# Slot steps and LoRA splits on GpSimd, and a new order at the start of z, in a quantized-weight and expert kernel

## What is computed

```python
lora_delta = lora_B @ lora_A * (LORA_ALPHA / LORA_RANK)
scale = jnp.exp(scale_log)
normalized = (weight + lora_delta).reshape(O, I // GROUP, GROUP) / scale
idx = jnp.searchsorted(thresholds, normalized, side='left')
quantized = cb[idx]
w_q = (quantized * scale).reshape(O, I)
x = x + x @ (w_q + lora_delta).T              # L0
W = weights[itok_B_0_15]
x = x + jnp.einsum('bct,bcd->bdt', x, W)      # L1
```

## Time and profile before

| | |
|---|---|
| median of 3 runs | 78.94 us (78.63 to 78.97) |
| the profiled execution | 78.95 us |
| its span | 77.1 us |
| granted TensorE clock | 1.0 in all slices |
| TensorE, VectorE, ScalarE, GpSimd busy | 71.6, 55.6, 47.3, 4.6 us |
| HBM read, written | 5.89 MB, 4.19 MB |

### The profile page before, as it was taken

The page is one execution under the profiler, slowest core; times in us unless marked ns, Lnnn a source line. Parts: engine busy times, 40 slices in busy tenths (PEclk is TensorE's granted clock), DMA queues, the critical chain, the costliest instruction groups (busy, mean ns, idle before and its releaser), DMA issues.

```text
span 77.1 us, 1130 instructions
## 1 busy us (share of the span) xinstructions
PE 71.6 (93%) x382; PEld 59.1 (77%) x382; DVE 55.6 (72%) x155; ACT 47.3 (61%) x73; POOL 4.6 (6%) x13
## 2 busy tenths in 40 slices
PE   4995987999999999999999999999999999999950
PEld 4921976986999978888878888878888878888940
DVE  4888999999999999999899998938998020000000
ACT  1945999687499998498349994359851341320420
POOL 4500000040000004000002000020000000000000
PEclk9999999999999999999999999999999999999999
DMA  1799999999200000003510305230315033033141
GB/s 17 184 300 356 382 398 393 389 356 219 79 0 0 0 0 0 0 0 136 210 70 0 136 4 187 85 136 0 136 62 210 11 125 135 10 136 136 48 156 68
DMA packets 5606, 10.16 MB, mean 132 GB/s; under 512 B 672, under 2 KB 960, under 8 KB 5600
## 3 DMA queue, kind: packets, MB, share of 16 engines
q1 hardware_dynamic: 5408, 10.03, 37.5%
q10 hardware_dynamic: 192, 0.06, 0.4%
HBM read 5.89 MB, written 4.19 MB: 131 GB/s over the span
## 4 chain that ended last, share of the span: by engine, by line
PE 77%; ACT 16%; issue 1%; DVE 1%; ACTq 0%
PE ps L481 57%; PE ps L452 7%; ACT blocks L342 5%; ACT z_hi L346 4%; PE ps L420 4%; ACT z_lo L351 4%; PE ps L504 2%; PE ps L459 2%; PE ps L470 2%; PE ps L428 1%; ACT blocks L340 1%; DVE turned_pick L590 1%; ACT la_hi L386 1%; ACT lbt_hi_lo L388 1%; ACT m_hi L372 1%
## 5 line engine op out<-in xcount | busy, mean ns | idle before, releaser
L481 PE MATMUL ps<-z_lo,m_hi 128*128 128x512 f32 (+1 forms) x68 | 17.6, 381 | 0.1
L481 PE MATMUL ps<-z_hi,m_lo 128*128 128x512 f32 (+1 forms) x68 | 17.7, 381 | 0.0
L481 PE MATMUL ps<-z_hi,m_hi 128*128 128x512 f32 (+1 forms) x68 | 17.4, 377 | 0.0
L452 PEld LDWEIGHTS ps<-blocks,x_sb 128*128 128x128 f32 x128 | 15.1, 192 | 2.7 <-issue 2.4
L452 PE MATMUL ps<-blocks,x_sb 128*128 128x128 f32 x128 | 15.6, 276 | 0.8 <-ACT blocks L340 0.8
L377 ACT ACTIVATE x_sb<-ps 128x512 f32<-128x512 f32 x15 | 8.9, 591 | 11.7 <-PE ps L481 11.7
L481 PEld LDWEIGHTS ps<-z_lo,m_hi 128*128 128x128 f32 x68 | 12.1, 188 | 3.1 <-ACT m_hi L372 0.9
L481 PEld LDWEIGHTS ps<-z_hi,m_hi 128*128 128x128 f32 x68 | 12.4, 188 | 2.4
L481 PEld LDWEIGHTS ps<-z_hi,m_lo 128*128 128x128 f32 x68 | 12.2, 189 | 2.2
L367 ACT ACTIVATE lift<-jump,top_step 128x512 f32<-128x512 f32 x18 | 12.3, 721 | 2.0 <-DVE jump L704 1.7
L704 DVE SCALAR_TENSOR_TENSOR jump<-norm,top,lift 128x512 f32<-128x512 f32 x18 | 12.9, 755 | 0.6 <-ACT lift L367 0.3
(11 more groups left out here) (88 smaller groups left out, 60.7 us busy)
## 6 DMA issues: line engine op xcount, KB each, us to landing
x_sb<-in_x SPq DMA_DIRECT2D x8, 512.0 KB, 8.3
out<-x_sb SPq DMA_DIRECT2D x15, 256.0 KB, 2.5
w_sb<-in_weight SPq DMA_DIRECT2D x4, 256.0 KB, 8.1
lora_sb<-in_lora SPq DMA_DIRECT2D x2, 256.0 KB, 7.8
out<-x_sb SPq DMA_DIRECT2D x2, 128.0 KB, 1.9
halves<-in_experts SPq DMA_DIRECT2D x1, 64.0 KB, 2.0
levels_sb<-in_levels ACTq DMA_DIRECT2D x1, 40.0 KB, 2.0
tok_sb<-in_tokens ACTq DMA_DIRECT2D x1, 16.0 KB, 2.2
```

The costliest lines, as they stand in the source:

```text
L452: last = nc.tensor.matmul(z_bank(r)[:, g], x_sb[:, r, g * P:(g + 1) * P], blocks[:, r], start=(g == 0), stop=False, skip_group_check=True)
L481: last = nc.tensor.matmul(dst, mm[:, u, g * P:(g + 1) * P], zz[:, g, n_cols], start=(k == 0), stop=(k == 3 * G - 1))
```

## The change

- TensorE: the LoRA of tile 1 stands ahead of z, those of tiles 2 and 3 behind products 2 and 5. Tile 0 is turned inside the last z pair, between its two row groups.
- Blocks: six row groups are early instead of four, so the late ones are wanted by pair 3. Which engine clears what stays (`CLEAR_RT`). ScalarE fills two of the four late pieces ahead of its first high part of z and two behind it.
- Slots: VectorE makes the steps of two slots (`OWN_SLOTS`), GpSimd those of the other six: six compares, a product with `step_up`, and sums over halves of the width. VectorE signals `step_up_ready` and waits for `rest_known` ahead of step 2 of tile 0.
- LoRA splits: on GpSimd, behind the identity of tile 1.
- Order of VectorE: `add_lora(2)`, `make_fixed(2)` and `low_m(1)` stand ahead of tile 2's steps, `make_fixed(3)` ahead of tile 3's. ScalarE normalises tile 2 behind `high_m(1)`.

```diff
+OWN_SLOTS = 2
-EARLY_RT = 4
+CLEAR_RT = 4
+EARLY_RT = 6
-LORA1_AFTER = 3
-TURN0_AFTER = 6
+LATE_FIRST = 2
+LORA_AT = {2: 2, 5: 3}
...
+            def split_lora():
+                low_rows = slice(R, 2 * R)
+                pool.wait_ge(lora_hi_ready, 2)
+                nc.gpsimd.tensor_tensor(la_lo[:], la_sb, la_hi[:].bitcast(F32), ALU.subtract).then_inc(lora_lo_ready, 1)
+                pool.wait_ge(lora_lo_ready, 1)
+                nc.gpsimd.tensor_tensor(lbt_hi_lo[low_rows], lbt_sb[low_rows], lbt_hi_lo[low_rows].bitcast(F32),
+                                        ALU.subtract).then_inc(lora_lo_ready, 1)
+                pool.wait_ge(lora_lo_ready, 2)
+
+            rest = SLOTS - OWN_SLOTS
+            each = [P, rest, L]
+            pool.wait_ge(step_up_ready, 1)
+            for s in range(OWN_SLOTS, SLOTS):
+                nc.gpsimd.tensor_scalar(match[:, s], key[:], top[:, s:s + 1], None, ALU.is_equal
+                                        ).then_inc(slots_matched, 1)
+            pool.wait_ge(slots_matched, rest)
+            nc.gpsimd.tensor_tensor(match[:, OWN_SLOTS:SLOTS], match[:, OWN_SLOTS:SLOTS],
+                                    step_up[:].rearrange("p (o l) -> p o l", o=1).broadcast_to(each),
+                                    ALU.mult).then_inc(slots_matched, 1)
+            pool.wait_ge(slots_matched, rest + 1)
+            width = L // 2
+            summed = rest + 1
+            while width > 1:
+                nc.gpsimd.tensor_tensor(match[:, OWN_SLOTS:SLOTS, 0:width], match[:, OWN_SLOTS:SLOTS, 0:width],
+                                        match[:, OWN_SLOTS:SLOTS, width:2 * width], ALU.add).then_inc(slots_matched, 1)
+                summed += 1
+                pool.wait_ge(slots_matched, summed)
+                width //= 2
+            nc.gpsimd.tensor_tensor(top_step[:, OWN_SLOTS:].rearrange("p (s o) -> p s o", o=1),
+                                    match[:, OWN_SLOTS:SLOTS, 0:1], match[:, OWN_SLOTS:SLOTS, 1:2], ALU.add
+                                    ).then_inc(rest_known, 1)
...
                 for u in range(OC):
                     complete(u)
                     pool.sem_inc(fixed_ready, 1)
+                    if u == 1:
+                        split_lora()
...
-            for q in range(PB):
+
+            def place_late(q):
                 nc.scalar.activation(own_block(q, late), turned_block(q, late), ACT.Copy).then_inc(late_blocks_ready, 1)
+
+            for q in range(LATE_FIRST):
+                place_late(q)
...
             for p in range(PAIRS - 1):
                 high_z(p)
+                if p == 0:
+                    for q in range(LATE_FIRST, PB):
+                        place_late(q)
...
-            normalize(2)
             copy_out(1)
             copy_out(2)
             for u in range(1, OC):
                 high_m(u)
+                if u == 1:
+                    normalize(2)
...
+                    if r == RT - 2:
+                        turn(0)
                 last.then_inc(z_ready, 1)
...
             lora(0)
+            lora(1)
...
-                if p == LORA1_AFTER:
-                    lora(1)
-                if p == TURN0_AFTER:
-                    turn(0)
             for n in range(N_OUT - 1):
                 product(n)
-                if n in (0, 2):
-                    lora(2 + n // 2)
+                if n in LORA_AT:
+                    lora(LORA_AT[n])
...
+            need(max(b, k1))
+            dve.sem_inc(step_up_ready, 1)
...
-            for s in range(SLOTS):
+            for s in range(OWN_SLOTS):
...
                     if s + 1 < SLOTS:
+                        if s + 1 == OWN_SLOTS:
+                            dve.wait_ge(rest_known, 1)
                         ahead = step_over(s + 1)
...
-            quantize_by_chains(1, {0: lambda: low_and_fix(1), 1: lambda: low_z(PAIRS - 2), 2: add_lora_and_low_z})
-            quantize_by_chains(2, {0: lambda: fix_and_low(2), 2: lambda: add_lora(3)})
-            quantize_by_chains(3, {0: lambda: fix_and_low(3)})
+            quantize_by_chains(1, {0: low_and_fix, 1: lambda: low_z(PAIRS - 2), 2: lambda: low_z(PAIRS - 1)})
+            add_lora(2)
+            make_fixed(2)
+            low_m(1)
+            quantize_by_chains(2, {2: lambda: add_lora(3)})
+            make_fixed(3)
+            quantize_by_chains(3, {0: lambda: low_m(2)})
             low_m(3)
```

More of the change, by code:

```diff
@@ L159, in build @@
         levels_counted = sem("levels_counted")
+        step_up_ready = sem("step_up_ready")
+        slots_matched = sem("slots_matched")
+        rest_known = sem("rest_known")
         scaled = sem("scaled")
@@ L330, in _ @@
             nc.scalar.activation(minus_ident[:], ident[:], ACT.Copy, scale=-1.0).then_inc(minus_ready, 1)
-            nc.scalar.activation(blocks[:, late], ident[:].rearrange("p (o n) -> p o n", o=1
-                                                                     ).broadcast_to([P, RT - EARLY_RT, P]),
+            nc.scalar.activation(blocks[:, CLEAR_RT:], ident[:].rearrange("p (o n) -> p o n", o=1
+                                                                          ).broadcast_to([P, RT - CLEAR_RT, P]),
                                  ACT.Copy, scale=0.0).then_inc(late_blocks_clear, 1)
@@ L441, in make_z @@
                     pe.wait_ge(blocks_clear, 1)
+                    pe.wait_ge(late_blocks_clear, 1)
                     pe.wait_ge(blocks_ready, PB)
                 if p == EARLY_RT // 2:
-                    pe.wait_ge(late_blocks_clear, 1)
                     pe.wait_ge(late_blocks_ready, PB)
@@ L543, in _ @@
             V.memset(halves[HP:], 0.0).then_inc(unused_rows_clear, 1)
-            V.memset(blocks[:, early], 0.0).then_inc(blocks_clear, 1)
+            V.memset(blocks[:, 0:CLEAR_RT], 0.0).then_inc(blocks_clear, 1)
             dve.wait_ge(kinds_numbered, 1)
@@ L592, in _ @@
                     dve.wait_ge(blocks_clear, 1)
+                    dve.wait_ge(late_blocks_clear, 1)
                     dve.wait_ge(pick_turned, 1)
@@ L719, in _, with low_and_fix @@
             normalize(1)
[L721 to L736, removed]
+            def low_and_fix():
+                low_m(0)
+                make_fixed(1)
             def low_z(p):
@@ L741, in low_z @@
                                 pair(z_hi, p).bitcast(F32), ALU.subtract).then_inc(last_z_lo_ready, 1)
-            def add_lora_and_low_z():
-                add_lora(2)
-                low_z(PAIRS - 1)
-            quantize_by_chains(1, {0: lambda: low_and_fix(1), 1: lambda: low_z(PAIRS - 2), 2: add_lora_and_low_z})
-            quantize_by_chains(2, {0: lambda: fix_and_low(2), 2: lambda: add_lora(3)})
-            quantize_by_chains(3, {0: lambda: fix_and_low(3)})
+            quantize_by_chains(1, {0: low_and_fix, 1: lambda: low_z(PAIRS - 2), 2: lambda: low_z(PAIRS - 1)})
[5 more added lines that the diff above has]
+            quantize_by_chains(3, {0: lambda: low_m(2)})
             low_m(3)
```

## The result

The changed kernel takes 81.72 us, against 78.86 before: ratio 1.0347, interval 1.0312 to 1.0382, **2.9 us slower** by the medians. One of its four runs (82.75 us) was in a slower state that executions of any kernel here fall into at times, and the ratio, which stands for 2.7 us, leaves such runs out. The profiled execution took 81.52 us with a span of 79.7, 2.6 more than before. I had forecast 78.7 in a range of 77.2 to 80.9.

What follows compares the result with a forecast made beforehand. TensorE was taken to bound up to 27.74 us, VectorE up to 39.22, then TensorE. From 78.95, less 0.87 at `eff` 1, plus 0.46 and 0.2 behind that turn, came 78.74, said as 78.7, range 77.2 to 80.9.

Steps and rivals of the forecast that it cites:

- What bounds the kernel: Bound taken as TensorE up to 27.74 us, VectorE's chain (slots, tile 0, tile 1) up to 39.22, TensorE alone after.
- z begins: Start of z on TensorE: z at about 7.8 us, first high part at 9.8, first product at 25.9, 1.8 earlier.
- When GpSimd is done: GpSimd's six slots, awaited by VectorE's step 2 of tile 0: done at 15.9 us, between 14.3 and 19.6.
- rival B: GpSimd's slot chain is slow and the kernel slower, deciding from 16.5 us; 80.5 if done at 17.7; chance 0.18.
- Tile 1: VectorE from `eff` 0 to `eff` 1: 12.7 us plus 0.55 for GpSimd's splits, ending at 38.35, 0.87 earlier.
- rival C: A GpSimd operation shuts VectorE out for its whole length; a split costs two-input steps 1.8 us; total 80.0; chance 0.15.
- Behind the turn: After tile 1's turn on TensorE: LoRA of tile 3 adds 0.46 us, the turn of tile 2 0.2, tile 3 nothing.

## Why the prediction was wrong

- **What bounds the kernel** was right: VectorE's chain up to the turn of tile 1. z alone gave nothing, and eight slots on VectorE gave back all.
- **z begins** 0.3 later than I said (8.08, and the first high part at 10.17 instead of 9.8). Most other traces with this start have it between 7.46 and 7.90, so the 0.3 is of this execution and not of the sum. Where VectorE's tile 0 is in time, with eight or four slots on VectorE, the first product starts at 25.96 to 26.31, against the 25.9 of my sum. That TensorE gains there is real, and VectorE does not let it through.
- **The step that failed is "When GpSimd is done"**: 18.14, not 15.9. Two of its terms were mis-sized. The six compares cost 2.56 instead of 1.1: the only one-input row of before was a select of 0.29 for 128 elements, and I went below its 1.75 for six; even that upper bound was too low. An upper bound from another kind of operation isn't one. Disturbance cost 1.27 instead of 0.25. I had written that VectorE "soon stands still", but it first does its normalising and first steps, just while the compares run; the upper bound, 1.2, was the right size. The seven two-input operations with their seven waits took 3.48 undisturbed, where I had 2.8 + 1.0: the operations 2.92, and the waits 0.56, because they are cheap (0.08 to 0.1, not 0.23). Short operations are not (0.2 for six elements). 1.46 + 1.02 − 0.32 + 0.08 for a later start are the 2.24. VectorE then stood for 3.27, beyond the 2.5 that I had named as the sign of rival B.
- **Tile 1**: `eff` 1 came 13.75 after `eff` 0, where I had 12.7 + 0.55. The splits cost 1.05. The first did fall on the low part of z, as argued; the second held up a step for 1.03. I had scaled the small delays (0.15, 0.2) by length; a delay does not follow the length (rival C, below).
- **Behind the turn**: 0.46 and 0.2 forecast, 0.46 and 0.25 measured; `eff` 2 ended 12.15 behind `eff` 1, forecast 12.1.
- The sum with the measured terms: 78.74 + 2.24 + 0.5 = 81.5, which is the profiled execution. It was rival B with its condition (done behind 16.5, each microsecond one on the end), with a term of rival C. I priced B's end at 17.7 and gave it 0.18; its terms as I wrote them add up to 17.5.
- **Rival C** was about a GpSimd operation that shuts VectorE out for its whole length. The traces bear it out, once one sees when the two start. In tile 1 of the changed kernel two of VectorE's steps met a GpSimd operation:

```profile
30.96 0.90 POOL L312 TENSOR_TENSOR fixed<-fixed,ident 128x128 f32<-128x128 f32 x1 [10.73 <-DVE fixed L702]
31.46 0.95 DVE L757 SCALAR_TENSOR_TENSOR jump<-norm,top,lift 128x512 f32<-128x512 f32 x1
...
33.65 1.71 POOL L320 TENSOR_TENSOR lbt_hi_lo<-lora_sb,lbt_hi_lo 64x512 fp32r<-64x512 f32 x1
34.13 1.78 DVE L757 SCALAR_TENSOR_TENSOR jump<-norm,top,lift 128x512 f32<-128x512 f32 x1
```

  The addition ends at 31.86 and its step at 32.41; the split ends at 35.36 and its step at 35.91. With four slots on GpSimd the product ends at 13.58 and the normalising at 14.12. Each time VectorE is through about 0.55 behind GpSimd. So the delay is what is left of GpSimd's operation when VectorE's instruction begins, less about 0.2: 0.40 left and 0.20 lost, 1.23 left and 1.03 lost. The small delays in the rows were this same hold, met near its end. This agrees with what the Trainium skill ("SBUF — State Buffer", "SBUF: two separate sides") states of the shared port pair, whose loser fully blocks. The same section of the Trainium skill limits this to VectorE instructions with two SBUF inputs or in a two-port mode, and the low part of z, with one input in PSUM, kept its 1.21. The first steps, which read one tile, take part too: the sixth compare was held beside two of them, and in tile 0 of the kernel before one took 0.69 instead of 0.54 beside the identity addition. Whether they run in such a mode no run shows.
- I also misread a row. The identity addition of 0.46 that I called undisturbed ran from 40.81 beside an instruction of VectorE that reads PSUM, in the kernel before:

```profile
40.65 0.68 DVE L656 TENSOR_TENSOR m_lo<-ps,m_hi 128x512 fp32r<-128x512 f32 x1
```

  Those of 0.84 and 0.90 met a sum and two steps that read two tiles in SBUF. Which of VectorE's instructions hold GpSimd up could be read before the change.
- The estimate of 2.9 for the seven from the Trainium skill ("GPSIMD Engine Reference", 3.1) was nearer to the measured 2.92 than my 2.8. The word of the same page of the Trainium skill (4.1) that one-input work is roughly line-rate does not hold for this compare (2.5 ns an element, more than the two-input product).

## What to carry to other kernels

Work that is moved to GpSimd off VectorE's path can cost VectorE three times: the signal (0.6 us here), the wait for the result, and each instruction that meets a GpSimd operation without reading PSUM (one with two inputs in SBUF then ended 0.55 us behind it). Count all three before the gain; of eight slots of 0.2 us neither six nor four were worth moving. If GpSimd must work beside VectorE, start it where VectorE reads PSUM: one wait did that here and was worth 0.9 us.

## What was not expected of the hardware

- A compare of GpSimd with one input, 64 elements on 128 partitions, takes 0.444 us, longer than a two-input product of the same size (0.322), and grows by 2.5 ns an element against 2.2.
- Dependent GpSimd operations start 0.08 to 0.1 us behind one another; the shortest one, of six elements, still takes 0.2.
- On VectorE, waiting for its own result and then signalling took 0.6 us in all, 0.26 of it behind the following instruction.
- An instruction of VectorE with 512 elements and two inputs in SBUF that meets a GpSimd operation ends about 0.55 us behind it, whether 0.4 or 1.2 us of that operation were left. Where VectorE's instruction had one input in PSUM, neither was held up (1.21 and 1.30 us).
